# Attention and feed-forward on one core: the first attention step's order on TensorE, ScalarE and the DMA queue

## The reference

```python
xn = _layernorm(x, axis=-1)                       # x: 16 batches, 256 tokens, 256 features
# attention: 16 heads of 16
qkv = (xn @ w_qkv).reshape(b, s, 3, HEADS, HEAD_DIM)
q, k, v = (qkv[:, :, 0], qkv[:, :, 1], qkv[:, :, 2])
scores = jnp.einsum('bqhd,bkhd->bhqk', q / scale, k)
scores = jnp.where(causal_mask[None, None], scores, NEG)
attn = jax.nn.softmax(scores, axis=-1)
out = jnp.einsum('bhqk,bkhd->bqhd', attn, v).reshape(b, s, HIDDEN) @ w_out
# feed-forward in fp8
outputs = _qdot(jax.nn.gelu(_qdot(xn, w_gating[0])) * _qdot(xn, w_gating[1]), w_linear)
x = x + out + outputs
```

## Time and profile before

| | |
|---|---|
| median of 3 runs | 366.3 us (364.39, 366.3, 366.59) |
| the profiled execution, its own time | 366.19 us |
| its span from first to last instruction | 364.5 us |
| granted TensorE clock, mean over the span | 0.972 of full |
| TensorE busy with matmuls | 341.3 us (94%) |
| VectorE busy | 298.5 us (82%) |
| ScalarE busy | 227.6 us (62%) |
| GpSimd busy | 168.2 us (46%) |

### The profile page before, as it was taken

How to read it: one execution, slowest core, us unless ns; L and a number is a source line. 1 busy time by engine, 2 the same in 40 slices (tenths; PEclk the granted TensorE clock), 3 DMA queues, 4 the chain that set the end, 5 groups by cost and what they waited for, 6 DMA issues and landing times.

```text
span 364.5 us, 9751 instructions
## 1 busy us (share of the span) xinstructions
PE 341.3 (94%) x3498; PEld 260.1 (71%) x3498; DVE 298.5 (82%) x1356; ACT 227.6 (62%) x368; POOL 168.2 (46%) x204
## 2 busy tenths in 40 slices
PE   7789999999999789999999999999999999979775
PEld 6336565666677678788788888888887888866454
DVE  5968988998425678999989999999999899996643
ACT  1655786667655376776676767766766767664540
POOL 2212333232235137456665575475566555753441
PEclk9969999999999999999999999999999999995889
DMA  7987655773248242534637528447355373250001
GB/s 251 323 287 224 183 151 141 175 232 123 77 142 298 65 145 90 201 120 150 193 112 225 167 97 263 120 144 246 104 179 195 112 222 118 91 206 30 32 29 59
DMA packets 46553, 57.59 MB, mean 158 GB/s; under 512 B 2664, under 2 KB 39080, under 8 KB 46504
## 3 DMA queue, kind: packets, MB, share of 16 engines
q1 hardware_dynamic: 46504, 56.96, 48.6%
HBM read 16.78 MB, written 12.58 MB: 81 GB/s over the span
## 4 chain that ended last, share of the span: by engine, by line
PE 81%; DVE 10%; ACT 3%; issue 2%; DMA 2%; SPq 0%; POOL 0%; DVEq 0%; ACTq 0%; POOLq 0%
PE ps L805 13%; PE ps L710 12%; PE ps L786 12%; PE ps L765 9%; PE ps L717 7%; PE ps L697 6%; PE ps L676 6%; PE ps L822 6%; PE ps L682 6%; DVE masked L457 3%; PE ps L814 2%; DMA xres<-in_L_attn_x_dram 2%; PE ps L661 2%; ACT arena L572 2%; DVE act L423 1%
## 5 line engine op out<-in xcount | busy, mean ns | idle before, releaser
L457 DVE CUSTOM_DVE_ANT_0 masked<-ps,causal 128x256 bf16<-128x256 f32 (+1 forms) x512 | 148.5, 353 | 21.1 <-PE ps L765 21.1
L572 ACT ACTIVATE arena<-ps 128x1024 f32<-128x1024 f32 x96 | 98.4, 1025 | 61.1 <-PE ps L786 61.0
L330 POOL TENSOR_SCALAR_AFFINE_SELECT arena<-arena 128x512 f32<-128x512 f32 (+1 forms) x96 | 73.6, 787 | 39.1 <-ACT arena L572 38.9
L304 POOL TENSOR_TENSOR qk_part<-w_raw,qk_part 128x512 fp32r<-128x512 f32 x32 | 41.1, 1286 | 55.5 <-ACT qk_part L551 55.5
L527 ACT ACTIVATE gate<-ps 128x512 bf16<-128x512 f32 x64 | 38.5, 602 | 35.0 <-PE ps L676 32.6
L786 PE MATMUL ps<-stack 64*128 64x256 f32 (+1 forms) x512 | 53.0, 307 | 4.8 <-ACT arena L572 4.8
L805 PE MATMUL ps<-arena,v_aug 128*32 128x256 f32 (+1 forms) x1024 | 50.8, 341 | 2.9 <-DVE o_norm L474 2.8
L710 PE MATMUL ps<-xs,wq_part 128*128 128x256 f32 x384 | 52.3, 285 | 0.3 <-ACT w_raw L545 0.3
L765 PE MATMUL ps<-stack 63*128 63x256 f32 (+1 forms) x512 | 48.3, 288 | 3.2 <-DVE row_max L457 3.1
L786 PEld LDWEIGHTS ps<-stack 64*128 64x128 f32 x512 | 36.9, 190 | 18.7 <-issue 7.3
L710 PEld LDWEIGHTS ps<-xs,wq_part 128*128 128x128 f32 x384 | 47.5, 189 | 1.6 <-ACT w_raw L545 0.6
(11 more groups left out here) (60 smaller groups left out, 458.6 us busy)
## 6 DMA issues: line engine op xcount, KB each, us to landing
stack<-qk_part SPq DMA_DIRECT2D x96, 256.0 KB, 2.7
xt_store<-xt_part SPq DMA_DIRECT2D x16, 512.0 KB, 4.2
xs<-xt_store SPq DMA_DIRECT2D x16, 512.0 KB, 4.2
out_dram<-w_raw SPq DMA_DIRECT2D x16, 256.0 KB, 4.1
xres<-in_L_attn_x_dram SPq DMA_DIRECT2D x7, 512.0 KB, 6.7
arena<-in_L_ffn_w_gating_dram SPq DMA_DIRECT2D x2, 1024.0 KB, 8.9
stack<-zeros SPq DMA_DIRECT2D x4, 512.0 KB, 7.5
arena<-in_L_ffn_w_linear_dram SPq DMA_DIRECT2D x1, 1024.0 KB, 12.9
```

What stands on the lines that cost most here:

```text
L304: nc.gpsimd.tensor_tensor(qk_part[:, g, QLO:KLO + 1:3, :], qk_raw[:, g, :, :], qk_part[:, g, QHI:KLO, :].bitcast(F32), ALU.subtract).then_ ...
L330: nc.gpsimd.affine_select(diag, diag, pattern=[[0, 1024 // width], [1, P]], compare_op=ALU.is_ge, fill=0.0, base=0, channel_multiplier=-1) ...
L457: last = nc.vector.tensor_tensor_reduce(masked[:, place, i * width:(i + 1) * width], max_ps[:, place, i * width:(i + 1) * width], causal[: ...
L572: nc.scalar.activation(arena[:, n, :, :], exp_ps, ACT.Exp).then_inc(exp_done, 1)
```

## The change

In step 0 the work is the same and its order another.

- TensorE: two `down` pieces stand behind each of M0 to M3, where four stood behind M0 and four behind M1. `project_v(1)` moves from ahead of M2 to between M4 and M5, and `project_qk(2, 0)` from ahead of M5 to behind it.
- ScalarE: `negate_max(0, 0)` stands between the two last `copy_ffn`, and `round_qk(2, 0)` ahead of `exponent(0, 0)`.
- SyncE: the DMA of the first negated maxima, `place_max(0, 0)`, is issued ahead of `load_xs(3)`.

```diff
--- before.py
+++ after.py
@@ -253,11 +253,14 @@
                     place_max(s - 1, 1)
                 if s >= 1 and has(s + 1):
                     fill_stack(s + 1, 0)
+                if s == 0:
+
+                    place_max(0, 0)
                 if has(s + 3):
                     load_xs(s + 3)
                 if has(s - 4):
                     store_y(s - 4)
-                if has(s):
+                if s >= 1 and has(s):
                     place_max(s, 0)
             for i in range(2):
                 sp.wait_ge(y_stored[i], 16 * (B // 2))
@@ -616,19 +619,23 @@
                         evacuate_v(0)
             copy_ffn(CHUNKS - 2, 1)
 
-            for s in range(B + 4):
+            copy_ffn(CHUNKS - 1, 0)
+            negate_max(0, 0)
+            copy_ffn(CHUNKS - 1, 1)
+            evacuate_v(1)
+            copy_qk(2, 0)
+            round_qk(2, 0)
+            exponent(0, 0)
+            for s in range(1, B + 4):
                 if has(s - 1):
                     negate_max(s - 1, 1)
                     exponent(s - 1, 1)
                 if has(s - 3):
                     round_ot(s - 3, 1)
-                if s >= 1 and has(s + 1):
+                if has(s + 1):
                     copy_qk(s + 1, 1)
                 if has(s - 1):
                     exponent(s - 1, 2)
-                if s == 0:
-                    for i in range(2):
-                        copy_ffn(CHUNKS - 1, i)
                 if has(s + 1):
                     evacuate_v(s + 1)
                 if has(s - 1):
@@ -825,32 +832,40 @@
                 last.then_inc(ot_used, 1)
 
             pe.wait_ge(gelu_done, J * CHUNKS)
-            for s in range(B + 4):
+
+            for n in range(4):
+                max_scores(0, n)
+                down(CHUNKS - 1, 2 * n)
+                down(CHUNKS - 1, 2 * n + 1)
+
+            pe.wait_ge(qk_copied[1], 2)
+            transpose_max(0, 0)
+            max_scores(0, 4)
+            pe.wait_ge(v_done, 1)
+            project_v(1)
+            max_scores(0, 5)
+            pe.wait_ge(neg_done[0], 1)
+            project_qk(2, 0)
+            for s in range(1, B + 4):
                 if has(s - 1):
                     exp_scores(s - 1, 0)
                 if has(s):
                     max_scores(s, 0)
-                if s == 0:
-                    for piece in range(4):
-                        down(CHUNKS - 1, piece)
                 if has(s - 1):
 
                     pe.wait_ge(*((y_done, s - 3) if s >= 4 else (v_done, s + 1)))
                     transpose_max(s - 1, 1)
-                if s >= 1 and has(s + 1):
+                if has(s + 1):
 
                     pe.wait_ge(qk_copied[0], s + 2)
                     project_qk(s + 1, 1)
                 if has(s):
                     max_scores(s, 1)
-                if s == 0:
-                    for piece in range(4, 8):
-                        down(CHUNKS - 1, piece)
                 if has(s - 1):
                     exp_scores(s - 1, 1)
                 if has(s + 1):
 
-                    pe.wait_ge(*((neg_done[1], s) if s >= 1 else (v_done, 1)))
+                    pe.wait_ge(neg_done[1], s)
                     project_v(s + 1)
                 if has(s - 1):
                     exp_scores(s - 1, 2)
```

## The result

| | before | changed |
|---|---|---|
| median of 20 runs | 366.18 us (361.95 to 368.74) | 362.13 us (360.94 to 364.35) |
| ratio | | 0.9916, 95% interval 0.9895 to 0.9937 |
| profiled execution, own time | 366.19 us | 362.20 us |
| span | 364.5 us | 360.5 us |
| mean granted clock of the profiled execution | 0.972 | 0.991 |

A forecast was written before the change was run, and what follows sets the result against it. The prediction took TensorE and VectorE starving in turn in step 0 as the bound: 2.0 us saved on TensorE, cut to 1.5 by ScalarE; 366.19 less 1.5 gives 364.7 us, range 362.7 to 366.6.

The forecast's parts named there:

- What bounds the kernel: TensorE and VectorE starve in turn in step 0; TensorE is full from 160 to 320 us, so early gains last.
- ScalarE takes part back: Copy, rounding, table load and X0 make E1 wait 0.7 us, cutting TensorE's 2.0 us saving to 1.5.
- if X0 turned out not to bind: Upper bound of the gain, 2.1 us, should ScalarE's X0 not hold up E1.
- The reordered projection costs nothing by itself: Late project_qk(2, 0) in step 0 was costed at nothing, as X0 was 1.2 us early.
- The queues: Four effects of moved orders, on place_max, the last copy_ffn, load_xs(3) and GpSimd's Q/K split, all costed at nothing.
- The sum: Whole time: 366.19 us of the profiled execution less the 1.5 us gain is 364.7 us.
- that one stretch stays at 2.4 GHz: Rival in the tail: a times_v stretch that ran slow before keeps full clock, giving 361.3 us; 6 in 100.
- The rival of the table load: Ahead of X0 on ScalarE, the load costs 2 x 1.28 us; gain only 0.2 us, time 366.0; 4 in 100.

The follow-up runs named there:

- e1: Kernel before with only the down pieces spread two behind each of M0 to M3; projections, ScalarE and SyncE orders unchanged; ratio to before 0.9954.
- e2: Changed kernel with the down pieces back to four and four behind M0 and M1, late projections kept; ratio to before 1.0034.
- e3: Changed kernel with round_qk(2, 0) moved back behind exponent(0, 0) on ScalarE; ratio to before 0.9926.
- e4: Changed kernel with an unused 4-column exponential behind the last GELU, so the table load comes early; ratio to before 0.9924.
- e6: e1 with negate_max(0, 0) moved ahead of the last copy_ffn and evacuate_v on ScalarE; ratio to before 0.9923.
- e9: Changed kernel with place_max(0, 0) put back behind load_xs(3) on SyncE; a single execution of 361.80 us.
- a_again: Changed kernel run once more, unaltered, beside runs of the kernel before on the same chip; 362.31 us, ratio to before 0.9940.
- e7: Kernel before with 6, 5 and 3 dummy transposes in TensorE's three waits of steps 0 and 1; ratio to before 0.9991.
- e8: e4 with 3 to 8 dummy transposes in each of six TensorE waits of steps 14 to 16; 360.62 us, ratio to before 0.9838.

## Why the prediction was right in one part and short in another

**What bounds the kernel.** Right, and shown by e1 and e2. VectorE starved behind M1 and TensorE after that; the pieces between the units cured both, and M1 to M5 start within 0.11 us of the computed places. The steady part carried the gain to the end unchanged: `times_v(12, 1)` starts 316.68 - 314.91 = 1.77 us sooner, of which 0.48 is M0's start and 1.29 steps 0 and 1.

**ScalarE takes part back.** Right, and shown by e3 and e4: the wait of E1 on X0 was computed at 0.7 and is 0.46, both cures end at 13.68. The rounding is 0.63 of it, against the 0.61 that was said. The gain at E1 was computed at 1.5 and is 1.39. The bound of 2.1 "if X0 turned out not to bind" is 2.02 in e3 and e4.

**"The reordered projection costs nothing by itself."** The runs bear it out. With the rounding behind X0 in both, the kernel with late projections (e3) is 0.47 us ahead of the one with early ones (e6) at E1 and 0.05 at E2, and not behind it. But the rounding ahead of X0 took away more than they give: as a whole, the change ends 0.16 us behind e6 at E1 and 0.27 at E2.

**The queues.** All four were costed at nothing, and no wait appeared. But I had not priced the other side: with V late, SyncE's move is what keeps E0 from waiting 1.4 us (e9). And the negation's move, which I treated as one of several without effect, is worth 0.75 us where the projections are early (e6 against e1); in the changed kernel's own order it was not undone.

**The sum.** This is the step that fell short: "366.19 us of the profiled execution less 1.5 is 364.7". The measured change is 3.1 us. The median of 362.13 lies 0.6 us under the low end of the range, while the ratio applied to the 366.3 us of before gives 363.2, inside it. That this lies inside is partly luck, since only half of the 3.1 us is the computed gain. Two things were wrong with the sum. Its base was one execution with a mean clock of 0.972, where the 57 runs of before have 0.9809. And the clock had no term: the changed kernel's 29 runs have 0.9859, a difference of 0.0050 ± 0.0024, which at 2.1 us per 0.01 is 1.1 us beside the 1.70 ± 0.27 at equal clock. The clock was in the forecast only as a rival ("that one stretch stays at 2.4 GHz", 361.3 us, 6 in 100). In the profiled pair two thirds of that case came about: 2.15 us of the 3.4, and with the 0.48 us ahead of M0 the computed 364.7 becomes 362.1, where 362.20 was measured.

**Whether the order raises the mean clock** is not settled. On the two chips that both were run on, the 49 runs of e1, e3, e4, e6 and a_again have 0.9840 and the 42 of before 0.9818, a difference of 0.0022 ± 0.0024, which chance can make. The falls of the first chunk come in both orders and can't be the change's doing, and half of the clock difference between the two profiled executions is one of them. Falls in steps 0 and 1, seen in three traces of other orders and in none of seven of the new one, are a part that fits, but filling the same waits in the kernel before (e7) didn't move the time by more than 1.6 us on one side or 0.9 on the other, with 0 in between. The fall at 328 us was 10 us long in two of the four traces of before's order with E1 at 15.7, and in one of seven of the new; too few to say more. What e8 adds is that with the waits of the tail filled both falls there are absent from its one trace.

**The rival of the table load** is refuted. The rows of the changed kernel have X0 1.29 us behind the load's start, and in e3, where a copy stands ahead of the load and not a rounding, it starts 1.30 us behind it. The Trainium skill's drain of 1.38 us for a switch ("ScalarE: Activation LUTs", What ACT_TABLE_LOAD costs) shows in neither trace.

## What to carry to other kernels

When one engine has filler work and another takes turns with it over a few buffers, spread the filler in portions of the partner's time for one unit; two portions of four pieces starved both engines, and four portions of two left VectorE waits of 0.16 and 0.52 us where it had 0.64 and 2.23. Then walk the chain behind it on every engine: here a negation of 0.37 us in the wrong place took back 0.75, a one-time table load or a rounding on the path 0.6, and 8 KB behind a 512 KB load 0.8. Judge such changes by distances between named instructions in one trace, which repeat to 0.02 us, and treat the mean clock as a second result with its own scatter. And compare two kernels that differ in one thing: the late projections looked like a loss against e6 until e3 was set beside it.

## What the runs showed of the hardware that was not expected

- With dummy transposes of 0.11 us each in waits of 0.4 to 1.2 us, TensorE's clock stayed at the upper level through the tail of one trace, where all other traces but one show two falls, and that one shows one. The Trainium skill ("TensorE: Matmul & The Clock Gate", Part 4) says that a transpose doesn't count as PE-busy in the same way. The trace of e8 speaks against it, with 1.00 in the windows from 320 to 348 us, though only in one trace, and in it transposes stand among matmuls and never alone.
- An 8 KB transfer issued 0.37 us behind one of 512 KB on the same queue took 3.0 us to land instead of 1.5 or less.
- The whole time of a run follows its mean granted clock at 2.1 us per 0.01, with 0.6 us of scatter, over runs that differ by 9 us. But lower clock doesn't cost the same everywhere: the fall of 6.8 us in the first chunk, 0.009 of the mean, goes with an M0 that starts 1.2 us later on average (114.69 us in seven traces, 113.48 in five without a fall there), where the line would have 2.0 (6.8 x 0.5 / 364.5 of mean clock, times 2.1 us per 0.01).
